# A selective scan on one core: z's second block in another PSUM bank, ScalarE's copies of the convolution two steps later, and the last blocks of x and z through silu straight from PSUM

## The reference

```python
def _mamba(x, in_w, conv_w, conv_b, xproj_w, dt_w, dt_b, A_log, D, out_w):
    xz = jnp.einsum('bld,ed->ble', x, in_w)
    xi, z = jnp.split(xz, 2, axis=-1)
    xi = jax.nn.silu(_dw_conv(xi, conv_w, conv_b))          # 4 taps along the sequence
    xdb = jnp.einsum('bld,ed->ble', xi, xproj_w)
    dtr, Bm, Cm = (xdb[..., :DTR], xdb[..., DTR:DTR + DS], xdb[..., DTR + DS:])
    dt = jax.nn.softplus(jnp.einsum('blr,dr->bld', dtr, dt_w) + dt_b)
    y = _selective_scan(xi, dt, Bm, Cm, -jnp.exp(A_log), D)  # h = exp(dt A) h + dt x B;  y = C h
    y = y * jax.nn.silu(z)
    return jnp.einsum('bld,ed->ble', y, out_w)
```

## Time and profile before

| | us |
|---|---|
| median of 3 runs | 1076.92 (1074.68 to 1078.11) |
| the profiled execution | 1075.14 |
| its span, first to last instruction | 1073.4 |
| the scan stage within it, first scan to last gate | 549.9 to 997.3 |

### The profile page before, as it was taken

The page is one execution under the profiler, slowest core; times in us unless marked ns, Lnnn a source line. Parts: engine busy times, 40 slices in busy tenths (PEclk is TensorE's granted clock), DMA queues, the critical chain, the costliest instruction groups (busy, mean ns, idle before and its releaser), DMA issues. The chain is left out here.

```text
span 1073.4 us, 13094 instructions
## 1 busy us (share of the span) xinstructions
PE 952.4 (89%) x3836; PEld 600.2 (56%) x3836; DVE 853.7 (80%) x1117; ACT 562.8 (52%) x1128; POOL 689.5 (64%) x378
## 2 busy tenths in 40 slices
PE   5898867999999999996969897899989997787798
PEld 2566646888888888885524432443434342232587
DVE  3688767777777777776748899999988999999853
ACT  2687732333333333332866777676776667564141
POOL 3377723555555555652159999899989999999000
PEclk9899988999999999999979989899989998989899
DMA  3000024352342343321245655556456655554001
GB/s 104 1 2 0 1 113 144 107 156 79 103 149 90 103 139 99 105 74 51 54 120 147 168 169 167 125 149 182 150 144 145 163 147 161 154 168 124 0 1 39
DMA packets 60031, 115.30 MB, mean 107 GB/s; under 512 B 10400, under 2 KB 15776, under 8 KB 59856
## 3 DMA queue, kind: packets, MB, share of 16 engines
q1 hardware_dynamic: 58848, 112.87, 37.6%
q10 hardware_dynamic: 1136, 1.90, 0.6%
HBM read 113.24 MB, written 1.51 MB: 107 GB/s over the span
## 5 line engine op out<-in xcount | busy, mean ns | idle before, releaser
L1731 POOL TENSOR_TENSOR uB<-u,rows_B 128x1024 f32<-128x1024 f32 x127 | 298.7, 2363 | 0.0
L870 POOL TENSOR_TENSOR lutw<-lutw,lt 128x865 f32<-128x865 f32 x80 | 184.8, 2310 | 164.6 <-DVE lt L836 158.9
L1970 PE MATMUL ya<-hV,ident 128*128 128x512 f32 x320 | 179.6, 649 | 48.3 <-DVE hV L1850 41.0
L1950 DVE TENSOR_TENSOR_SCAN da<-da,uB 128x512 f32<-128x512 f32 x160 | 193.5, 1220 | 14.7 <-ACT da L1835 13.6
L1741 POOL TENSOR_TENSOR hP<-hS,rows_C 128x512 f32<-128x512 f32 x96 | 122.2, 1273 | 26.7 <-PE ya L1970 14.9
L1970 PEld LDWEIGHTS ya<-hV,ident 128*128 128x128 f32 x320 | 58.3, 199 | 138.7 <-DVE hV L1850 90.1
L1947 DVE TENSOR_TENSOR_SCAN hS<-da,uB 128x512 f32<-128x512 f32 x96 | 116.0, 1208 | 14.4 <-ACT da L1835 8.9
L744 ACT ACTIVATE ah<-ups 128x1024 fp32r<-128x1024 f32 x40 | 41.1, 1029 | 130.0 <-DVE ups L832 130.0
L1850 DVE TENSOR_TENSOR hV<-da,rows_C 128x512 f32<-128x512 f32 x160 | 106.8, 668 | 0.0
L1970 PE MATMUL ya<-hP,ident 128*128 128x512 f32 x192 | 102.3, 615 | 0.0
L829 DVE TENSOR_TENSOR si<-gps,cwb 128x1024 f32<-128x1024 f32 x40 | 49.0, 1225 | 57.0 <-ACT gps L741 53.2
(11 more groups left out here) (357 smaller groups left out, 2052.7 us busy)
## 6 DMA issues: line engine op xcount, KB each, us to landing
rows_B<-bc_rows SPq DMA_DIRECT2D x128, 256.0 KB, 3.6
rows_C<-bc_rows SPq DMA_DIRECT2D x128, 256.0 KB, 4.4
wr<-in_moe_w SPq DMA_DIRECT2D x40, 384.0 KB, 4.5
cwb<-cw_rows SPq DMA_DIRECT2D x16, 512.0 KB, 4.0
cwb<-cw_rows SPq DMA_DIRECT2D x16, 384.0 KB, 4.4
cwb<-cw_rows SPq DMA_DIRECT2D x16, 256.0 KB, 3.9
lut_f<-in_lut_idx SPq DMA_DIRECT2D x1, 2160.0 KB, 10.0
cwb<-cw_rows SPq DMA_DIRECT2D x16, 128.0 KB, 4.1
```

Source lines behind the costliest of these rows:

```text
L870: e.tensor_tensor(part, part, lt[:, q, :], ALU.add).then_inc(s_la, 1)
L1731: e.tensor_tensor(uB[:, r % UPAIRS, :, :], u[:, d:d + 2, :], RB[:, r % BROWS, :].unsqueeze(1).broadcast_to([P, 2, HALF]), ALU.mult).then_i ...
L1950: e.tensor_tensor_scan(a[:, way], a[:, way], uB[:, r % UPAIRS, b, way], 0.0, ALU.mult, ALU.add).then_inc(s_sc, 1)
L1970: return e.matmul(ya[n % 2][:, :], g.ident[:, :], at, start=False, stop=False, skip_group_check=True).then_inc(done, 1)
```

## The change

Four things. Segment 1's second block of z goes to bank S1 and its third to S2 (before: S2 and S1), with the waits exchanged, and its dues become 25, 27, 33, 35 (before: 24, 26, 28, 33). ScalarE's copies out of S1 come two steps later, TensorE's convolutions one. `copy_conv` of the last block is gone: `silu_x` reads S1 itself, then the other three blocks. In segments 2 and 3 `copy_z` of the last block is gone and `silu_z` reads the bank. Around these, many dues move by one or two.

```diff
-        GZ = [[ya[0], ya[1], da[1], da[2]], [S0, S2, S1, S0], [S2] * DB, [S2] * DB]
+        GZ = [[ya[0], ya[1], da[1], da[2]], [S0, S1, S2, S0], [S2] * DB, [S2] * DB]
...
             yield from due_from(0, x_tensor(e, k, 0))
-            if k > 1:
-                yield 2
-                dt_tensor(e, k - 1, 2)
             yield 3
             yield from due_from(3, x_tensor(e, k, 1))
+            if k > 1:
+                yield 4
+                dt_tensor(e, k - 1, 2)
             yield 5
...
-            yield 8
-            yield from due_from(8, x_tensor(e, k, 2))
-            yield 10
+            yield 9
+            yield from due_from(9, x_tensor(e, k, 2))
+            yield 11
...
                 elif m == 1:
+                    e.wait_ge(s_cv, DB)
+                elif m == 2:
                     e.wait_ge(s_u, DB)
                     e.wait_ge(s_dtc, DB)
-                elif m == 2:
-                    e.wait_ge(s_cv, DB)
...
             if k == 1:
-                yield from gate_tensor(e, k, [24, 26, 28, 33])
+                yield from in_turn(gate_tensor(e, k, [25, 27, 33, 35]), begun(36, rows_tensor(e, k, 36)), dt_tensors(e, k))
...
         def silu_x(e, k):
+
+            m = DB - 1
+            e.wait_ge(s_c, DB * k)
+            e.activation(xi[:, k % 2, m, :], S1[:, :], ACT.Silu).then_inc(s_cv, 1)
             e.wait_ge(s_cv, DB * k)
-            e.activation(xi[:, k % 2, :, :], xi[:, k % 2, :, :], ACT.Silu).then_inc(s_xi, 1)
+            e.activation(xi[:, k % 2, 0:m, :], xi[:, k % 2, 0:m, :], ACT.Silu).then_inc(s_xi, 1)
...
         def silu_z(e, k):
-            e.wait_ge(s_zc, DB * (k + 1))
-            e.activation(sz[:, k % 2, :, :], sz[:, k % 2, :, :], ACT.Silu).then_inc(s_sz, 1)
+
+            n = DB if k == 1 else DB - 1
+            e.wait_ge(s_zc, DB * k + n)
+            e.activation(sz[:, k % 2, 0:n, :], sz[:, k % 2, 0:n, :], ACT.Silu).then_inc(s_sz, 1)
+            if k > 1:
+                e.wait_ge(s_z, DB * (k + 1))
+                e.activation(sz[:, k % 2, n, :], GZ[k][n][:, :], ACT.Silu).then_inc(s_zc, 1)
...
-            yield 13
+            yield 15
             copy_conv(e, k, 0)
             newest_tap(e, k, 1)
-            yield 15
+            yield 16
             copy_x(e, k, 2)
-            yield 18
+            yield 20
             copy_conv(e, k, 1)
...
-            yield 28
-            copy_conv(e, k, 3)
-            yield 31
+            yield 32
             keep_dt(e, k - 1, 3)
             yield 33
             silu_input(e, k)
...
-            yield 49
+            yield 48
             copy_low_rank(e, k)
...
-                yield 49
+                yield 51
                 split_vector(e, 0)
```

More of the change, by code:

```diff
@@ L1168, in project_tensor @@
             yield from due_from(5, conv_tensor(e, k, 0))
-            yield 8
-            yield from due_from(8, x_tensor(e, k, 2))
-            yield 10
+            yield 9
+            yield from due_from(9, x_tensor(e, k, 2))
+            yield 11
             if k > 1:
                 sum_tensor(e, k - 1, 2)
-                yield 10
-            yield from due_from(10, conv_tensor(e, k, 1))
-            yield 13
-            yield from due_from(13, x_tensor(e, k, 3))
-            yield 15
-            yield from due_from(15, conv_tensor(e, k, 2))
-            yield 18
+                yield 12
+            yield from due_from(11, conv_tensor(e, k, 1))
+            yield 14
+            yield from due_from(14, x_tensor(e, k, 3))
+            yield 16
+            yield from due_from(16, conv_tensor(e, k, 2))
+            yield 19
             dt_tensor(e, k - 1, 3)
-            yield 20
-            yield from due_from(20, conv_tensor(e, k, 3))
-            yield 23
+            yield 21
+            yield from due_from(21, conv_tensor(e, k, 3))
+            yield 24
             sum_tensor(e, k - 1, 3)
@@ L1211, in rows_tensor @@
             if k == 1:
-                e.wait_ge(s_zc, DB + 3)
+                e.wait_ge(s_zc, DB + 2)
             for q in range(DB):
@@ L1322, in side_tensor @@
             yield from project_tensor(e, k)
-            yield 24
+            yield 25
             if k == 1:
-                yield from gate_tensor(e, k, [24, 26, 28, 33])
+                yield from in_turn(gate_tensor(e, k, [25, 27, 33, 35]), begun(36, rows_tensor(e, k, 36)), dt_tensors(e, k))
             else:
-                yield from out_tensor(e, seg - 1, 0, 24)
+                yield from out_tensor(e, seg - 1, 0, 25)
                 yield 33
                 yield from out_tensor(e, seg - 1, 1, 33)
-            yield 36
-            yield from rows_tensor(e, k, 36)
-            if k > 1:
+                yield 36
+                yield from rows_tensor(e, k, 36)
                 yield from in_turn(dt_tensors(e, k), begun(44, gate_tensor(e, k, [44, 48, 53, 57])))
-            else:
-                yield from dt_tensors(e, k)
         def split_scalar(e, i):
@@ L1378, in skip @@
                 e.wait_ge(s_xi, DB + seg)
+                e.wait_ge(s_cv, DB * seg)
                 e.wait_ge(s_g, 2 * pair - 1 + b)
@@ L1504, in first_gate_scalar @@
         def first_gate_scalar(e):
-            for due, m in ((31, 0), (36, 1), (37, 2)):
+            for due, m in ((32, 0), (34, 1), (39, 2), (41, 3)):
                 yield due
@@ L1509, in first_scalar, with first_rows_scalar @@
         def first_scalar(e):
-            yield from in_turn(first_block_scalar(e), project_scalar(e, 1), first_gate_scalar(e))
+            yield from in_turn(first_block_scalar(e), project_scalar(e, 1), first_gate_scalar(e), first_rows_scalar(e))
+        def first_rows_scalar(e):
             yield 38
@@ L1558, in begin_scalar @@
             e.preload_act_table_set("natural_log_exp_and_others")
-            yield 9
+            yield 11
             parts(e, seg, 2)
-            yield 11
+            yield 12
             exp(e, seg, 2)
-            yield 12
+            yield 13
             log(e, seg, 2)
-            yield 20
+            yield 22
             keep_dt(e, seg, 2)
@@ L1588, in middle_scalar @@
             exp(e, k, 0)
+            yield 54
             parts(e, k, 1)
-            yield 54
+            yield 55
             exp(e, k, 1)
-            yield 55
             log(e, k, 0)
             yield 56
+            copy_z(e, k, 1)
+            yield 57
             log(e, k, 1)
-            yield 56
-            copy_z(e, k, 1)
             yield 60
@@ L1650, in side_vector @@
             k = seg + 1
-            yield 17 if seg else 10
+            yield 18 if seg else 10
             input_vector(e, seg, 2)
@@ L1655, in side_vector @@
                 out_vector(e, seg - 1, 0)
-            yield 28
+            yield 29
             input_vector(e, seg, 3)
             if seg == 0:
-                yield 49
+                yield 51
                 split_vector(e, 0)
-                yield 54
+                yield 55
                 split_vector(e, 1)
@@ L1857, in gate @@
                     e.wait_ge(s_ap, pool_steps(last))
-                    e.wait_ge(s_sz, seg) if seg else e.wait_ge(s_zc, DB)
+                    e.wait_ge(s_zc, DB * (seg + 1))
+                    if seg:
+                        e.wait_ge(s_sz, seg)
                     e.tensor_tensor(sz[:, seg % 2, d, :], ya[b][:, :], sz[:, seg % 2, d, :], ALU.mult).then_inc(s_g, 1)
```

23 lines of the change are left out of this document (8 added, 15 removed).

## The result

The changed kernel takes 1086.47 us (median of four runs, 1084.65 to 1087.59); the kernel before, beside it on the same chip, 1076.64 (four runs, 1074.68 to 1078.11). The ratio is 1.0099, 95% interval 1.0085 to 1.0113: 9.8 us slower, where +2.6 was forecast and the range ended at 1084.5.

A forecast was written before the change was run, and what follows sets the result against it. TensorE was taken to bound the first pairs, GpSimd close behind. Segment 0 +1.8, dt's third matmul +0.6 and silu +0.2 made +2.6 us on the median 1076.92: 1079.5 us, range 1074.5 to 1084.5.

The forecast's parts named there:

- segment 0, first gates: First pair of segment 0: TensorE waits about 4.5 us at z's second block, then a slow clock; gate 3.8 us late.
- segment 0, second pair: Second pair of segment 0: VectorE's waits of 0.97 and 1.01 us go, giving back 2.0 us (bounds 0 and 2.5).
- later copies, segments 1 and 2: Copies out of S1 two steps later: most of the 2.33 us wait at 1.14 goes, the gate comes no sooner; gain 0.
- dt's third matmul, with its dues: Segments 1 and 2: moved into TensorE's full stretch, it delays the gate 0.86 us, of which 0.3 shows each; +0.6 us.
- silu straight from PSUM: Split silus: 0.1 us each after step 1 of segments 2 and 3, dropped copies 0; +0.2 us.
- The remaining moved dues: dt's Abs, Exp, Ln and the second block's parts at step 54: only waits with GpSimd or TensorE later change; 0, within 0.3.
- the rival by which this pair pays: Segment 0's second pair gives back no 2.0 us and loses another 1.3: +5.9 us, 1082.8, up to 1085; chance 0.15.
- TensorE's full stretch: Nearly the whole first pair of segment 1, TensorE busy 47.00 of 47.00 us; said to hide the removed waits.
- the 0.55 us of cover: Scan 1.34 in segment 1 waited 0.55 us for its exponential anyway, so only 0.3 of dt's 0.86 us would show.
- the wait of some 6 us: Sign in the profile: VectorE's first gates in segment 0 wait some 6 us, 2.90 before.
- A gate wait of 1 to 1.5 us in segment 1: Sign: with no wait at 1.14 or under 0.5 us, the gate's wait grows to 1 to 1.5 us.
- a gate that waits no longer: Sign of a wrong prediction: segment 1's gate shows no longer wait though the one at 1.14 has gone.

The follow-up runs named there:

- run 4: Kernel before with only the later copies out of S1 and the new order of x blocks and convolutions on TensorE; 1073.37 us, ratio 0.9968.
- run 7: run 4 plus the other bank alone: in segment 0 z's second block goes to S1, its third to S2; 1072.42 us, ratio 0.9961.
- run 12: run 11 with dt's third matmul ahead of x's second block again and dt's Abs, Exp, Ln, copy and product due as before; 1075.64 us, ratio 0.9998.
- run 5: run 4 plus dt's third matmul behind x's second block in segments 1 and 2, with the dues that go with it; 1074.92 us, ratio 0.9983.
- run 11: Changed kernel with the convolution's fourth block again copied out of S1 at due 28 and x's silu whole; 1080.80 us, ratio 1.0044.
- run 6: run 4 plus both silus split, both last copies left out, z's third and fourth blocks behind the pair's last add in segment 0; 1073.12 us, ratio 0.9978.
- run 1: Changed kernel with the last segment's five dues for dt's third block put back as before; 1080.68 us, ratio 1.0047.
- run 2: Kernel before with one number changed: the copy of dt's third block due 22 instead of 20 in the last segment; 1078.97 us, ratio 1.0030.
- run 3: Changed kernel with z's second block in segment 0 behind the first pair's last add (dues 25, 33, 35, 37); 1082.66 us, ratio 1.0066.
- run 8: run 4 with two of the three convolution matmuls of each x block left out in segments 1 and 2; 1067.33 us, ratio 0.9920.
- run 9: run 7 with ScalarE's copy of x's first block due 5 instead of 7 in segments 1 and 2; 1065.73 us, ratio 0.9911.
- run 10: run 9 with the first copy due 4 and the second due 8 instead of 10 in segments 1 and 2; 1065.86 us, ratio 0.9901.

## Why the prediction was wrong

| step | forecast | measured |
|---|---|---|
| segment 0, first gates | +3.8 | +3.9 at the gate, +4.1 at step 36 |
| segment 0, second pair | -2.0 | -0.9 |
| later copies, segments 1 and 2 | 0 | -1.5 (run 4), -0.9 (run 7), -0.1 (run 12) |
| dt's third matmul, with its dues | +0.6 | +1.4 (run 4 to 5), +1.3 (run 11 against 12) |
| silu straight from PSUM | +0.2 | +0.2 (run 6, segments 1 to 3), no more than two executions differ |
| "The remaining moved dues" | 0, within 0.3 | +5.0, all in segment 3 |

**The step that failed** is the last: "The remaining moved dues [...] change waits in which GpSimd or TensorE is the later: 0, within 0.3". It was argued from segments 1 and 2, where TensorE's dues moved along. In the last segment `side_tensor` has a list of its own that the diff doesn't touch, and there the copy of dt moved past the matmul that waits for it. Runs 1 and 2 show it from both sides. Without those 5.0 us the changed kernel takes 1080.7 (run 1), inside the range. That run is 4.6 us slower than the kernel before, where +2.6 was forecast; the other terms miss by the rest.

**First gates.** Right, by mechanism and price: a wait of TensorE of 4.90 us (4.5 forecast), a gate at 616.91 against 615.2 plus the 1.6 us by which this execution's stage starts late. Runs 7 and 11 show what the prediction left unsaid: neither the bank nor the block's new place is at fault, but dropping the copy at 28.

**Second pair.** Right in sign, half the size. The wait at step 46 goes, as forecast, but one of 1.36 us comes at step 49: ahead of its exponential stands ScalarE's copy of the low-rank dt, due at 48 (49 before), which waits 2.11 us for TensorE. In run 3, with three blocks of z behind the gate, the pair loses 2.1 us. So the rival by which this pair pays can come about, though it isn't what the changed kernel met.

**Later copies.** "TensorE's full stretch" is the right bound (run 8). But I took from it that nothing before the stretch's end can help, and that needs the stretch to be full from its first microsecond. It begins with a wait of 2.08 us and then over 4 us at half pace, and that part can shift. Run 4 gains 1.5 us in these two segments, run 7 0.9, run 12 0.1, with the same copies. The granted clock tells them apart. The same stretch of segment 1, from 8.7 to 19.2 us after its first scan, in run 4 and in run 12:

```profile
671.90:682.40 10.50, 6.65 (x14) 3.55 (x15) 10.50 (x13) 8.21 (x18) 9.80 (x6) 0.84 0.50 120
```

```profile
672.50:683.00 10.50, 7.62 (x12) 3.91 (x13) 10.50 (x13) 7.72 (x17) 9.44 (x5) 0.51 0.54 118
```

Run 7 has 0.67 there and the kernel before 0.52. Read from the granted clock in each trace, in both segments: how long after the segment's first scan TensorE is back at full clock (us), and the shift of step 32 within the segment:

| | segment 1: full clock after, shift | segment 2: full clock after, shift |
|---|---|---|
| kernel before | 18.8, 0 | 18.9, 0 |
| run 4 | 17.4, -1.0 | 18.5, -0.4 |
| run 7 | 18.1, -0.6 | 18.7, -0.3 |
| run 12 | 19.1, -0.1 | 19.2, 0.0 |
| run 5, dt moved | 17.5, 0.0 | 17.5, 0.0 |
| run 3, dt moved | 17.5, 0.0 | 17.4, -0.2 |
| changed kernel, dt moved | 19.2, +0.9 | 18.2, +0.3 |
| run 11, dt moved | 19.1, +0.8 | 18.4, +0.4 |

Among runs with the same code the shift follows the clock: full pace 1.7 us sooner is worth about 1 us. Read at the 18.8 of the kernel before, the copies' own gain is some 0.2 us a segment; this is an estimate between the rows of runs 7 and 12. So the forecast of 0 was nearly right, and most of what run 4 gains is the earlier return of the clock. Whether the new order makes that return more likely, these single executions do not show.

**dt's third matmul.** The term was mis-sized. At the same return of the clock the runs with and without the move lie 0.8 to 1.1 us apart in a segment (run 5 and run 4 in segment 1, run 11 and run 4 in segment 2, run 11 and run 12 in segment 1). That is the pair of matmuls, 0.86 us, that the prediction began with; the 0.55 us of cover that it took off at scan 1.34 were not there, since the scan waits 0.58 us there still. Part of it shows earlier than the forecast had it: at step 12, behind ScalarE's functions of dt. The dues of these functions moved with the matmul, and no run parts the two.

Of the forecast's tests, z's block after the silu, the clock under 0.9, and no wait at 1.14 and 0.46 came true, and the wait of some 6 us did in two parts. A gate wait of 1 to 1.5 us in segment 1 did not: it is 0.34 (0.16 before), and VectorE had its longer waits at steps 12 and 16 already. The prediction gave a gate that waits no longer as a sign of being wrong, and 0.18 us more is next to that: what VectorE gained at 1.14 was taken back two steps later, by way of GpSimd, and not at the gate. ("GpSimd ties the two together in between" stands in the prediction; the sum made no use of it.)

## What to carry to other kernels

When a due is moved in a helper that every segment calls, look up the queue that waits for it in each segment, above all in the last one, which often has its own list. Where an engine is full up to the point that sets the time, look at the wait at which its full stretch begins: a copy two steps earlier there was worth 3 us a segment (run 9), while waits removed inside the stretch were half or wholly paid back. And before a copy out of a buffer is dropped in favour of a later use, ask who takes the buffer next: the copy at 28 cost ScalarE 0.6 us and saved TensorE a wait of 4.9.

## What the runs showed of the hardware

The price of a wait of TensorE isn't fixed. After the same wait of 3.5 us, at the same place of the program, TensorE came back to full pace after 3.3 us in run 11, 4.3 in run 2, 6.4 in run 3 and 6.6 in the changed kernel. VectorE's wait that follows from it was 3.33, 3.48, 4.72 and 4.88 us. The two rows of run 11 from which the 3.3 us come:

```profile
924.69 2.04 PE L1242 MATMUL side<-dtr,wdt 128*128 128x512 f32 x2 [3.47 <-ACT dt L1446]
...
928.03 1.02 PE L1262 MATMUL side<-sz,bm_w_o 128*128 128x512 f32 x2
```

Whether the clock falls at all can differ in the same way. Runs 7 and 10 have the same code in segment 0, and TensorE waits 1.70 us for the same product in both, just ahead of or inside this stretch:

```profile
618.00:622.00 4.00, 4.00 (x5) 0.78 (x6) 4.00 (x5) 3.95 (x11) 4.00 (x4) 0.57 0.64 167
```

```profile
618.00:622.00 4.00, 2.52 (x5) 0.73 (x6) 4.00 (x5) 3.96 (x11) 4.00 (x3) 1.00 0.42 45
```

Run 7 is granted 0.57, run 10 1.00, and segment 0 ends at -2.3 in run 7 and at -3.5 in run 10. A sum that rests on such a wait should carry 1.5 us of range for this alone; mine carried 2.2 for the first gate and nothing for the others, and a comparison of two single profiles carries the same uncertainty. Apart from it the stage repeats closely: at steps 8 and 12 of segment 0, ahead of which these kernels are alike, the starts in all profiled executions agree within 0.05 us.
